# Loading and splitting the first sixteen blocks of a graph layer in pieces of one or two blocks, on two queues

## What is computed

```python
def _L0_gnn_ref(x, adj, t, weight):
    ts = t[0]
    support = x @ weight
    return (1.0 - ts) * support + ts * (adj @ support)
x = _layernorm(x + _L0_gnn_ref(x, adj, L0_gnn_t, L0_gnn_weight), axis=-1)   # eps 1e-5, along the features
```

## Time and profile before

| | |
|---|---|
| median of 3 runs | 395.97 us (395.9 to 396.87) |
| profiled execution, device time | 395.5 us |
| its span in the profile | 393.7 us |
| TensorE busy | 379.0 us, 96% of the span |
| VectorE busy | 227.7 us, 58% |
| ScalarE busy | 143.8 us, 37% |
| GpSimd busy | 46.9 us, 12% |
| moved by DMA | 84.41 MB, mean 214 GB/s |

### The profile page before, as it was taken

The page is one execution under the profiler, slowest core; times in us unless marked ns, Lnnn a source line. Parts: engine busy times, 40 slices in busy tenths (PEclk is TensorE's granted clock), DMA queues, the critical chain, the costliest instruction groups (busy, mean ns, idle before and its releaser), DMA issues.

```text
span 393.7 us, 4192 instructions
## 1 busy us (share of the span) xinstructions
PE 379.0 (96%) x1737; PEld 315.7 (80%) x1737; DVE 227.7 (58%) x277; ACT 143.8 (37%) x101; POOL 46.9 (12%) x21
## 2 busy tenths in 40 slices
PE   5999999999999999999999999999999999999972
PEld 3778888888888888888888888888888888888862
DVE  2499967634775446933666445763378345684025
ACT  4776342432433335233243235233342323423010
POOL 3599420010000100001000100001000010000000
PEclk9999999999999999999999999999999999999997
DMA  7999996565665664566645657547555666610001
GB/s 255 422 422 390 338 382 218 214 229 168 245 216 167 261 247 170 208 234 234 219 189 195 237 203 267 212 162 268 187 197 203 217 224 252 210 57 2 0 1 53
DMA packets 17810, 84.41 MB, mean 214 GB/s; under 512 B 1792, under 2 KB 6144, under 8 KB 9728
## 3 DMA queue, kind: packets, MB, share of 16 engines
q1 hardware_dynamic: 17520, 83.89, 58.0%
q10 hardware_dynamic: 272, 0.26, 0.2%
HBM read 79.95 MB, written 4.19 MB: 214 GB/s over the span
## 4 chain that ended last, share of the span: by engine, by line
PE 90%; DVE 4%; DMA 3%; SPq 1%; issue 1%; ACT 1%; DVEq 0%
PE agg L324 28%; PE agg L326 28%; PE agg L325 28%; DMA a_raw<-in_adjT 3%; DVE a_lo L236 2%; PE out_ps L365 2%; PE out_ps L367 2%; PE out_ps L366 2%; DVE w_lo L303 1%; ACT a_hi L174 0%; SPq L136 0%; DVE x_raw L264 0%; SPq L107 0%; DVE x_raw L289 0%; DVE z_lo L255 0%
## 5 line engine op out<-in xcount | busy, mean ns | idle before, releaser
L236 DVE TENSOR_TENSOR a_lo<-a_raw,a_hi 128x2048 fp32r<-128x2048 f32 x63 | 155.0, 2467 | 129.0 <-ACT a_hi L174 129.0
L324 PE MATMUL agg<-a_hi,x_hi 128*128 128x512 f32 x512 | 200.6, 392 | 4.1 <-DVE a_lo L297 3.3
L325 PE MATMUL agg<-a_lo,x_hi 128*128 128x512 f32 x512 | 200.3, 391 | 0.0
L326 PE MATMUL agg<-a_hi,x_lo 128*128 128x512 f32 x512 | 200.0, 391 | 0.0
L174 ACT ACTIVATE a_hi<-a_raw 128x2048 fp32r<-128x2048 f32 x63 | 120.7, 1915 | 146.4 <-PE agg L326 138.9
L324 PEld LDWEIGHTS agg<-a_hi,x_hi 128*128 128x128 f32 x512 | 96.7, 189 | 25.5 <-issue 3.9
L326 PEld LDWEIGHTS agg<-a_hi,x_lo 128*128 128x128 f32 x512 | 96.7, 189 | 20.2
L325 PEld LDWEIGHTS agg<-a_lo,x_hi 128*128 128x128 f32 x512 | 96.7, 189 | 19.9
L220 POOL TENSOR_TENSOR xt<-xt,omt_col 128x1024 f32<-128x1024 f32 x8 | 18.6, 2324 | 261.6 <-DMA xt<-in_xT 261.6
L214 POOL TENSOR_TENSOR x_lo<-x_raw,x_hi 128x1024 fp32r<-128x1024 f32 x8 | 27.5, 3457 | 11.1 <-ACT x_hi L166 11.1
L181 ACT ACTIVATE z_hi<-z 128x512 fp32r<-128x512 f32 x16 | 10.1, 633 | 45.3 <-DVE z L249 45.3
(11 more groups left out here) (22 smaller groups left out, 49.0 us busy)
## 6 DMA issues: line engine op xcount, KB each, us to landing
a_raw<-in_adjT SPq DMA_DIRECT2D x63, 1024.0 KB, 4.8
x_raw<-in_x SPq DMA_DIRECT2D x8, 512.0 KB, 6.4
xt<-in_xT SPq DMA_DIRECT2D x8, 512.0 KB, 5.7
rows<-in_x SPq DMA_DIRECT2D x8, 512.0 KB, 5.6
out<-x_raw SPq DMA_DIRECT2D x7, 512.0 KB, 3.0
a_raw<-in_adjT SPq DMA_DIRECT2D x4, 256.0 KB, 6.0
out<-x_raw SPq DMA_DIRECT2D x4, 128.0 KB, 1.8
w_raw<-in_W ACTq DMA_DIRECT2D x1, 256.0 KB, 4.4
```

The lines of the kernel that those rows point to most:

```text
L236: nc.vector.tensor_tensor(a_lo[:, slot], a_raw[:, slot], a_hi[:, slot].bitcast(f32), ALU.subtract).then_inc(a_lo_ready[slot], 1)
L324: nc.tensor.matmul(bank, x_hi[:, j, cols], a_hi[:, slot, b], start=first, stop=False)
L325: nc.tensor.matmul(bank, x_hi[:, j, cols], a_lo[:, slot, b], start=False, stop=False)
L326: return nc.tensor.matmul(bank, x_lo[:, j, cols], a_hi[:, slot, b], start=False, stop=last)
```

## The change

The blocks of the first chunk are cut into pieces (first block, number of blocks). Six pieces have one block, five have two (these eleven, `RING_PIECES`, cover groups 0 to 3), and the last four are whole groups. Each piece of x and of adj gets a load of its own with a semaphore of its own, and each is split by itself.

- Queues: ACT's queue issues the adj pieces 0 to 3 and no weight load; SP's queue issues x of every piece, adj of pieces 4 to 10, `t` after piece 5, the weight after piece 8.
- High parts of x move from ACT (an activation) to DVE (`tensor_copy`), ahead of `a_lo` of the same piece. ACT makes `a_hi` only, then `w_hi` after all eleven pieces. `w_lo` and `omt_col` on DVE come after x_hi of piece 11 and ahead of `a_lo` of group 4.
- TensorE runs 8 matmuls on zeros instead of 9. For block 0 it runs the two high products as soon as both high parts are there, then the two with `a_lo`, then the two with `x_lo`. For each other piece it waits for both low parts.
- The number and shape of matmuls of the real work, the bytes moved, and everything in chunks 1 to 7 stay the same.

```diff
-WARM = 9
+WARM = 8
+PIECES = ((0, 1), (1, 1), (2, 1), (3, 1), (4, 1), (5, 1), (6, 2), (8, 2), (10, 2), (12, 2), (14, 2),
+          (16, 4), (20, 4), (24, 4), (28, 4))
...
+            def load_x(p):
+                j, n = PIECES[p]
+                if j // GROUP >= X_RING:
+                    sp.wait_ge(x_lo_ready, piece_after((j // GROUP - X_RING + 1) * GROUP))
+                sp.dma_start(x_raw[:, j // GROUP % X_RING, j % GROUP:j % GROUP + n], x_sta[:, j:j + n]
+                             ).then_inc(x_loaded[p], 16)
...
             load_x(0)
-            for b in range(GROUP):
-                landed = a0_loaded[b] if b < GROUP - 1 else a_loaded[0]
-                sp.dma_start(a_raw[:, 0, b], adjT[0, :, b]).then_inc(landed, 16)
-            sp.dma_start(t_col[:, :], t.partition_broadcast(P)).then_inc(t_loaded, 16)
-            for g in range(1, GROUPS):
-                load_x(g)
-                load_adj(0, g)
+            load_x(1)
+            for p in range(2, len(PIECES)):
+                load_x(p)
+                if p >= 4 and p < RING_PIECES:
+                    load_adj_piece(p)
+                if p == 5:
+                    sp.dma_start(t_col[:, :], t.partition_broadcast(P)).then_inc(t_loaded, 16)
+                if p == 8:
+                    sp.dma_start(w_raw[:, :, :], W.rearrange("(k p) n -> p k n", p=P)).then_inc(w_loaded, 16)
+                if p >= RING_PIECES:
+                    load_adj(0, PIECES[p][0] // GROUP)
...
-            act.dma_start(w_raw[:, :, :], W.rearrange("(k p) n -> p k n", p=P)).then_inc(w_loaded, 16)
+            for p in range(4):
+                load_adj_piece(p)
             act.preload_act_table_set("sqrt_and_others")
-            x_high(0)
...
-            for g in range(1, GROUPS):
-                x_high(g)
+            for p in range(RING_PIECES):
+                a_high_piece(p)
+            act.wait_ge(w_loaded, 16)
+            nc.scalar.activation(w_hi[:, :, :], w_raw[:, :, :], ACT.Copy).then_inc(w_hi_ready, 1)
+            for g in range(RING, GROUPS):
                 a_high(0, g)
...
+            def x_high(p):
+                j, n = PIECES[p]
+                dve.wait_ge(x_loaded[p], 16)
+                nc.vector.tensor_copy(x_hi[:, j:j + n], x_raw[:, j // GROUP % X_RING, j % GROUP:j % GROUP + n]
+                                      ).then_inc(x_hi_ready, 1)
...
+            for p in range(len(PIECES)):
+                x_high(p)
+                if p < RING_PIECES:
+                    a_low_piece(p)
                 else:
-                    dve.wait_ge(a_hi_ready[0], 1)
...
+                    if p == RING_PIECES:
+                        dve.wait_ge(w_hi_ready, 1)
+                        nc.vector.tensor_tensor(w_lo[:, :, :], w_raw[:, :, :], w_hi[:, :, :].bitcast(f32), ALU.subtract
+                                                ).then_inc(w_lo_ready, 1)
+                        dve.wait_ge(t_loaded, 16)
+                        nc.vector.tensor_scalar(omt_col[:, :], t_col[:, :], -1.0, 1.0, ALU.mult, ALU.add
+                                                ).then_inc(omt_ready, 1)
+                    a_low(0, PIECES[p][0] // GROUP)
...
+            def first_piece():
                 pe.wait_ge(x_hi_ready, 1)
+                pe.wait_ge(a0_hi_ready, 1)
+                for k in range(KT):
+                    nc.tensor.matmul(agg[0][k][:, :], x_hi[:, 0, k * P:(k + 1) * P], a_hi[:, 0, 0],
+                                     start=True, stop=False)
+                pe.wait_ge(a0_lo_ready, 1)
+                for k in range(KT):
+                    nc.tensor.matmul(agg[0][k][:, :], x_hi[:, 0, k * P:(k + 1) * P], a_lo[:, 0, 0],
+                                     start=False, stop=False)
+                pe.wait_ge(x_lo_ready, 1)
+                for k in range(KT):
+                    nc.tensor.matmul(agg[0][k][:, :], x_lo[:, 0, k * P:(k + 1) * P], a_hi[:, 0, 0],
+                                     start=False, stop=False)
+
+            def piece(p):
+                j, n = PIECES[p]
+                pe.wait_ge(a0_lo_ready, p + 1)
+                pe.wait_ge(x_lo_ready, p + 1)
+                for b in range(j, j + n):
                     for k in range(KT):
-                        done = products(0, 0, b, b, k, b == 0, False)
-                done.then_inc(a_used[0], 1)
+                        done = products(0, b // GROUP, b, b % GROUP, k, False, False)
+                if (j + n) % GROUP == 0:
+                    done.then_inc(a_used[j // GROUP], 1)
```

More of the change, by code:

```diff
@@ L26, in gnn_layernorm_kernel, with piece_after @@
     assert GROUPS == 2 * RING and KT == 2 and TILES == GROUP
+    RING_PIECES = sum(first < RING * GROUP for first, _ in PIECES)
+    def piece_after(blocks):
+        return sum(first < blocks for first, _ in PIECES)
     ctx = ExitStack()
@@ L103, in _, with load_adj_piece @@
         def _(sp):
[L104 to L108, removed]
+            def load_x(p):
[4 more added lines that the diff above has]
+                             ).then_inc(x_loaded[p], 16)
+            def load_adj_piece(p):
+                j, n = PIECES[p]
+                sp.dma_start(a_raw[:, j // GROUP, j % GROUP:j % GROUP + n],
+                             adjT[j // GROUP, :, j % GROUP:j % GROUP + n]).then_inc(a0_loaded[p], 16)
             def load_adj(c, g):
                 slot = g % RING
-                if turn(c, g):
-                    sp.wait_ge(a_lo_ready[slot], turn(c, g))
+                if turn(c, g) == 1:
+                    sp.wait_ge(a0_lo_ready, piece_after((slot + 1) * GROUP))
+                else:
+                    sp.wait_ge(a_lo_ready[slot], turn(c, g) - 1)
                 sp.dma_start(a_raw[:, slot], adjT[c * GROUPS + g]).then_inc(a_loaded[slot], 16)
@@ L163, in _, with load_adj_piece, a_high_piece @@
         def _(act):
[L164 to L167, removed]
+            def load_adj_piece(p):
+                j, n = PIECES[p]
+                act.dma_start(a_raw[:, j // GROUP, j % GROUP:j % GROUP + n],
+                              adjT[j // GROUP, :, j % GROUP:j % GROUP + n]).then_inc(a0_loaded[p], 16)
+            def a_high_piece(p):
+                j, n = PIECES[p]
+                act.wait_ge(a0_loaded[p], 16)
+                nc.scalar.activation(a_hi[:, j // GROUP, j % GROUP:j % GROUP + n],
+                                     a_raw[:, j // GROUP, j % GROUP:j % GROUP + n], ACT.Copy).then_inc(a0_hi_ready, 1)
             def a_high(c, g):
                 slot = g % RING
-                act.wait_ge(a_loaded[slot], 16 * (turn(c, g) + 1))
-                if turn(c, g):
-                    act.wait_ge(a_used[slot], turn(c, g))
+                act.wait_ge(a_loaded[slot], 16 * turn(c, g))
+                act.wait_ge(a_used[slot], turn(c, g))
                 nc.scalar.activation(a_hi[:, slot], a_raw[:, slot], ACT.Copy).then_inc(a_hi_ready[slot], 1)
@@ L211, in _, with x_low @@
         def _(pool):
[L212 to L216, removed]
+            def x_low(p):
+                j, n = PIECES[p]
+                pool.wait_ge(x_hi_ready, p + 1)
+                nc.gpsimd.tensor_tensor(x_lo[:, j:j + n], x_raw[:, j // GROUP % X_RING, j % GROUP:j % GROUP + n],
+                                        x_hi[:, j:j + n].bitcast(f32), ALU.subtract).then_inc(x_lo_ready, 1)
             def scale_xt(c):
@@ L224, in _ @@
             nc.gpsimd.memset(z_hi[:, 0].bitcast(f32), 0.0).then_inc(zeros_ready, 1)
-            for g in range(GROUPS):
-                x_low(g)
+            for p in range(len(PIECES)):
+                x_low(p)
             pool.wait_ge(omt_ready, 1)
@@ L234, in a_low @@
                 slot = g % RING
-                dve.wait_ge(a_hi_ready[slot], turn(c, g) + 1)
+                dve.wait_ge(a_hi_ready[slot], turn(c, g))
                 nc.vector.tensor_tensor(a_lo[:, slot], a_raw[:, slot], a_hi[:, slot].bitcast(f32), ALU.subtract
@@ L299, in _ @@
[L299 to L307, removed]
@@ L308, in _, with a_low_piece @@
-            dve.wait_ge(x_lo_ready, GROUPS)
+            def x_high(p):
+                j, n = PIECES[p]
+                dve.wait_ge(x_loaded[p], 16)
+                nc.vector.tensor_copy(x_hi[:, j:j + n], x_raw[:, j // GROUP % X_RING, j % GROUP:j % GROUP + n]
+                                      ).then_inc(x_hi_ready, 1)
+            def a_low_piece(p):
+                j, n = PIECES[p]
+                dve.wait_ge(a0_hi_ready, p + 1)
+                nc.vector.tensor_tensor(a_lo[:, j // GROUP, j % GROUP:j % GROUP + n],
+                                        a_raw[:, j // GROUP, j % GROUP:j % GROUP + n],
+                                        a_hi[:, j // GROUP, j % GROUP:j % GROUP + n].bitcast(f32), ALU.subtract
+                                        ).then_inc(a0_lo_ready, 1)
@@ L326, in products @@
                 return nc.tensor.matmul(bank, x_lo[:, j, cols], a_hi[:, slot, b], start=False, stop=last)
-            def first_group():
```

(22 more changed lines are left out.)

17 lines of the change are left out of this document (3 added, 14 removed).

## The result

| | before | after |
|---|---|---|
| median of 20 runs, us | 395.98 | 395.4 |
| ratio to before | | 0.998 (95%: 0.997 to 0.9989) |
| profiled execution, us | 395.5 | 394.82 |
| its span, us | 393.7 | 393.0 |
| first real matmul, us | 8.77 | 5.60 |

One of the 20 runs of the changed kernel took 2180.8 us; the ratio leaves it out, and nothing here tells its cause.

What follows compares the result with a forecast made beforehand. TensorE's gapless run from group 4 was taken as the bound: its start moves from 34.27 to 31.6 us, a gain of 2.7, giving 392.8 us profiled and 393.3 us median. Range 389.8 to 395.5, forecast's chance 0.50.

Steps and rivals of the forecast that it cites:

- What bounds the kernel: Whole kernel: its end moves by as much as the start of TensorE's gapless run, group 4 at 34.27 us before.
- First loads: Start: adj and x of block 0 land at 4.0 to 4.1 us, first real matmul at 4.85 instead of 8.77.
- my sum: Splitting up to group 4: the turns of DVE and POOL on all pieces add to 24.7 us, ending at 31.1.
- hand-overs: Between short instructions of the split: 0.5 us (0 to 1.5) added before group 4's start.
- The split: DVE and POOL up to group 4: copies and subtracts take turns, last to finish, so group 4 starts at 31.6 us.
- The clock at the start: TensorE's first real matmuls: they begin at half clock, and the clock rises near 7 to 9 us.
- Rival D: Wait before group 4, up to 3.9 us: clock falls again, costing 2.4 us; gain 0.3, 395.7 us; chance 0.08.
- it waits and the clock's rise is covered: Before group 4: TensorE could be there at 27.7 to 31.4 us, so waiting until 31.6 absorbs the slow start.
- A: Pieces up to group 4: x_hi copy runs beside POOL without taking turns; gain 5.7 us, 390.3 us; chance 0.24.
- C: Start: first pieces land late, at 6.1 us, shifting the chain by 2.0; gain 0.7, 395.3 us; chance 0.10.
- Nothing is late after that: After group 4: the next three pieces come every 5.0 us, under TensorE's 5.44, so no later wait.
- B: Pieces up to group 4: x_hi copy is slower and takes turns; middle 1.5 us lost, 397.5 us; chance 0.08.

Runs made afterwards that it cites:

- e4: Changed kernel with block 0's high products held back until both its low parts are there; 395.3 us, ratio 0.9965.
- e5: Changed kernel with 8 matmuls on zeros in the pause before group 4 and, in chunk 1, z of chunk 0 made one group sooner; 394.01 us, ratio 0.9942.
- r_after: The changed kernel itself run again, beside later kernels on the same chip; 395.17 us, ratio 0.9974.
- e1: Changed kernel with 8 matmuls on zeros put in TensorE's pause before group 4; 394.88 us, ratio 0.9966.
- e2: Changed kernel with all high parts of x made on ScalarE again, piece by piece; 391.03 us, ratio 0.987.
- e9: Changed kernel with only the high parts of x of groups 4 to 7 made on ScalarE; 393.58 us, ratio 0.9925.
- e3: Changed kernel with w_lo and omt_col made ahead of the last group's a_lo instead of group 4's; 394.12 us, ratio 0.9948.
- e10: The e2 kernel with 9 unused matmuls in TensorE's wait for z_lo before the last project; 390.25 to 390.87 us, ratio 0.9848.
- e11: The e2 kernel run again, beside e10 on the same chip; 390.77 and 391.68 to 391.93 us, ratio 0.9874.
- e6: The e2 kernel with x of blocks 0 to 3 loaded by one 512 KB transfer instead of four of 128 KB; 393.32 us, ratio 0.9925.

## Why the prediction was right and wrong, point by point

- *What bounds the kernel.* Right: in every kernel the ledger from group 4's start to the last z closes within 0.05 us once the returns are in it.
- *First loads.* Sizes off: adj of block 0 was ready for ACT at 4.83, not 4.0 to 4.1, and the first product at 5.60, not 4.85. From 1.5 to 4.5 us 180 GB/s moved, where the kernel before moved 266; I had carried over the old rate. That TensorE's first products came late cost nothing (e4). That the split began late did: `a_lo` of block 0 ended at 6.18, not 5.4, that of block 1 at 7.74, not 6.9, and that of group 4 at 31.94, where my sum has 31.1 before the hand-overs. It isn't only block 0: in e5's profile the turns of block 2 were 0.45 us ahead of the changed kernel's, then DVE waited 0.59 us for the high part of blocks 6 and 7, which ACT could begin only at 13.08 for want of its adj, and group 4 started at 32.00 again.
- *The split.* Right in its prices: the copy's middle price (0.28 and 0.68 alone) and its turns were as assumed, and a pair takes 2.57 us (forecast 2.62). That group 4 starts at 32.0 (31.6) is partly luck: the 0.5 us for hand-overs stood in for late loads, and the turns needed none of it. The profile's row with 0.41 for 256 columns was the wrong neighbour for a copy. Of the two pages cited in the prediction, the Trainium skill, "VectorE: DVE Perf Modes", section "The perf-mode tier table", has an f32 copy in SBUF at twice the plain rate, and the trace agrees: from 256 to 1024 columns it grows by 0.40 us, where a two-source subtract grows by 1.6 from 512 to 2048 (0.68 to 2.29), twice as much a column. The Trainium skill, "SBUF — State Buffer", section "Who interferes with whom", says that a copy at that rate and a GpSimd instruction exclude each other, and the trace agrees: 1.5 us where a copy of 512 stood behind `x_lo`.
- *The clock at the start.* I forecast its rise near 7 to 9. It came before the first real matmul here and in r_after, e1, e2, e5 and e9, and between 6.5 and 11.0 in the others with pieces, by the pace of the steps. In e4 the slow steps left group 4 where it was, as I had said of this rise.
- *Rival D* is what happened. I gave it 0.08 and put its place in "the wait before group 4"; its price was 1.7 us, not 2.4. The step of the forecast that failed is the one that "it waits and the clock's rise is covered", with nothing put down for what the wait itself does to the clock: the runs show a fall to 1.2 GHz after that wait of 1.87 us, worth 1.7 us, and none where the wait is filled (e1, e5). I counted a wait of TensorE as free time because the pace was set elsewhere; it is free only as long as the clock survives it. The pauses of 0.4 us in the earlier trace rows were no evidence for one of 1.9. That the measured 395.4 still lies inside my range is no credit to the forecast: the range was drawn wide for A and C.
- *"Nothing is late after that."* Wrong, and no rival had it: DVE's queue carries its delay to the first project, 0.49 to 0.95 us (e1, e3, e4), unseen in the changed kernel itself because the slow clock delayed TensorE too. I followed the pace of the splits (5.0 against 5.44) and left out DVE's wait for the last `x_lo` (2.30 us, none before), the scaled `xt`, which takes turns with DVE twice there, and z behind three `a_lo`. No run takes these three apart.
- *Rivals A, B, C.* A copy beside POOL (A), or one that is slow and takes turns (B), didn't happen. Of C there was 0.8 us, and it is in group 4's start: 0.8 us between my sum's 31.1 and 31.94.

## What to carry to other kernels

When a change moves the bound from the first operand's arrival to a helper engine, ask for each pause that the main engine then has whether its clock lasts through it, and fill it with throwaway matmuls if in doubt (e1, e5, e10). Before an operation is moved to relieve one engine, add up the turns on the engine that takes it together with those of the engine it alternates with: here ScalarE had room and VectorE with GpSimd had none, and moving the copies back was worth 4.4 us (e2). A gain that is returned once may be due to be returned again further on; close the first return before believing that it was the only one (e1, then e5).

## What the runs showed of the hardware that I had not expected

- TensorE's clock went from 2.4 to 1.2 GHz after pauses of 1.87 and 1.99 us with full work on both sides, and stayed at 2.4 after pauses of 1.25, 1.39 and 1.61 us. In the 2.28 us before the last project it fell in five of the profiled executions and held in the others, in the same code too (e2 and e11), so the length of a pause alone doesn't decide. When the granted clock falls varies too: 0.9 to 1.0 us after the restart at group 4 (the changed kernel and r_after), and from 0.15 us before to 1.1 us after the restart at the last project (e3, e9, e11, e4, e6). In each of these seven it is back after 3.4 us. What decides it within the same pause stays open. The row of the granted clock says nothing of the start: in the kernel before it shows 1.00 from 9 to 13 us, where the steps are 0.43 apart, so there only the pace tells.
- A cast from f32 to f32r on VectorE takes 0.28 to 0.29, 0.41 (e1, e4) and 0.68 us for 256, 512 and 1024 columns, and excludes GpSimd's subtract. The one-source subtract-and-multiply with two per-partition scalars takes 0.41 for 256; less the 0.14 of a one-column instruction, that is about twice the cast's time a column.
- One 512 KB transfer of x in front delayed the first high part of adj by 1.0 us and the next three by 2.7 to 3.4 us, against four transfers of 128 KB (e6 against e2).
